# Base registers loaded later, and another order in the setup, of a graph layer on one core

## The chip, the cores and the metric

The kernel runs on one core of a Trainium2 chip. The metric is device time in microseconds (us) of one execution; before the change the median of 3 runs is 811.84 us (811.63 to 813.36).

## The reference

Nodes N = 6250, features D = 128, edges E = 206250, sorted by dst. What is computed:

```
msg = x[src] + edge_attr                      # E x D
agg = segment_sum(msg, dst, num_segments=N)   # N x D
h   = relu(agg @ W1 + b1) @ W2 + b2
h   = (h - mean(h)) * rsqrt(var(h) + eps) * ln_w + ln_b     # over the whole of h
h   = graph norm over the nodes, per feature (gn_w, gn_b, gn_ms)
out = layernorm(x + (gelu(h) + x))            # per node
```

## The kernel before, in words

**Two sums make agg.** The sum of edge_attr over dst is made by groups of 3072 edges (68 groups, each in two halves): VectorE marks which node of a window of 32 an edge goes to (`mark`, L931), TensorE multiplies marks and edges (`sum_half`, L661), ScalarE copies the sums (L529), TensorE puts them at their place among 128 columns (`turn_sums`, L675, with the table `place` that `put` makes, L943), and `add` (L955) adds them on VectorE to `agg` at a column that comes from a register. The register is loaded by `base_of(g)` (L947), a `value_load` of one word of `base_i`, on VectorE's sequencer.

The sum of x[src] is made by 25 chunks of 250 nodes. For a chunk, a matrix of counts (250 nodes by N source nodes) is built: VectorE makes five batches of marks (`mark_batch`, L1020, two tables each, three batches of buffers), TensorE counts in 25 banks of 5 products each through a ring of 4 PSUM banks (L710), ScalarE copies each bank into `counts` (L553), and when all 25 are copied TensorE multiplies 49 tiles of x, each in a high and a low part, with `counts` (L735, 98 products), and VectorE adds the result to `agg` (`add_chunk`, L1028). There is one `counts` buffer: the copies of the next chunk start after the last L735.

**Where a chunk's edges are** is looked up on the way: `stage_tile` (L880) gives a slot, GpSimd gathers `begins` from the list of edges `listed` in HBM (L449), `stage_row` (L978 to L982) gives a finer slot, GpSimd gathers `near` (L456), `make_keys` (L991 to L1005) makes keys, TensorE turns them (L690) and ScalarE copies them (L535), after which `mark_batch` may start on the chunk.

**The order** is written out by hand on every engine. The loop over pairs of chunks has on VectorE an even half and an odd half. The even half starts with `base_of` twice, then `put` twice, mark, batch 3, mark, batch 4, `add`, `make_keys`, `stage_tile`, marks, batches 0 and 1 of the next chunk, `add`, batch 2, `stage_row`, `add_chunk`. The odd half starts with `base_of` three times.

**The setup.** SyncE loads dst, then x (after src has landed), then edges. ScalarE issues the loads of the last word of each tile of 256 edges (`tile_end_i`, 805 words) and of src. VectorE and ScalarE compare the ends with the 3125 pairs of nodes (`search`, in three pieces of 4, 10 and 11 chunks, 7 comparisons each), and TensorE sums the comparisons (L633). VectorE's comparisons (piece 0) have a buffer each; ScalarE's (L508) share 3 buffers and wait for TensorE to have used them (`below_used`). VectorE packs src and dst (L893), after which ScalarE stores `listed` (L514 to L516). ScalarE splits x into its high part (L522) between pieces 1 and 2, VectorE the low part (L961).

Of the kernel before, what the change touches and what calls it, by code (L numbers as in the profile page):

```python
# [14 lines left out]
P = 128  # L15
# [54 lines left out]
EARLY = 4  # L70
BELOW = 3
# [8 lines left out]
def gnn_kernel(nc, x, src, dst, edge_attr, W1, b1, W2, b2, ln_w, ln_b, gn_w, gn_b, gn_ms, out):  # L80
# [36 lines left out]
    with ExitStack() as ctx:  # L117
# [14 lines left out]
        pair_row = nc.alloc_sbuf_tensor_at("pair_row", [P, NPAIR + 7], I16, offset=counts_at)  # L132
        x_hi = sb("x_hi", [P, NT, D], F32R)
# [11 lines left out]
        below = behind[:, 0:BELOW * SEARCH * PAIRS].rearrange("p (s v) -> p s v", s=BELOW)  # L145
# [108 lines left out]
        below_ready = sem("below_ready")  # L254
        below_used = sem("below_used")
# [228 lines left out]
        def _(act):  # L484

            act.wait_ge(rows_padded, 1)
# [6 lines left out]
            act.dma_start(src_rows[0:EVEN, :], src_full[0:EVEN, :]).then_inc(src_loaded, 16)  # L493
            act.dma_start(src_rows[EVEN:FULL, :], src_full[EVEN:FULL, :]).then_inc(src_loaded, 16)
            act.dma_start(src_rows[FULL:GROUPS, 0:REST], src_rest).then_inc(src_loaded, 16)
# [4 lines left out]
            def search(piece, sets):  # L500

                a, b = PIECES[piece]
                act.wait_ge(ends_ready, 1)
                act.wait_ge(pair_row_ready, piece + 1)
                for i in sets:
                    n = piece * SETS + i
                    act.wait_ge(below_used, max(SETS, n + 1 - BELOW))
                    nc.scalar.activation(below[:, n % BELOW, 0:(b - a) * PAIRS], pair_row[:, a * PAIRS:b * PAIRS],  # L508
                                         ACT.Sign, bias=tile_bias[:, i:i + 1]).then_inc(below_ready, 1)

            search(1, range(EARLY))
# [6 lines left out]
            search(1, range(EARLY, SETS))  # L518
# [5 lines left out]
            search(2, range(SETS))  # L524
# [99 lines left out]
        def _(pe):  # L624
            def search(piece):

                a, b = PIECES[piece]
                for i in range(SETS):
                    n = piece * SETS + i
                    pe.wait_ge(below_ready, n + 1)  # L630
                    for c in range(a, b):
                        of = first_below[:, i] if piece == 0 else below[:, n % BELOW]
# [200 lines left out]
        def _(dve):  # L833
# [23 lines left out]
            dve.wait_ge(ends_loaded, 32)  # L857
            link(dve.tensor_scalar(tile_end[:, :], tile_end_i[:, :], 1.0 / PAIR, None, ALU.mult), setup, steps)
            link(dve.tensor_scalar(tile_bias[:, :], tile_end[:, :], -1.0, -0.25, ALU.mult, ALU.add), setup, steps)
            dve.engine_nop().then_inc(ends_ready, 1)  # L860

            def search(piece):

# [465 lines left out]
```

## Time and profile before

| | |
|---|---|
| median of 3 runs | 811.84 us |
| the profiled execution's own time | 805.35 us |
| its span | 803.0 us |
| mean granted clock of TensorE | 0.963 |
| busy: TensorE, VectorE, ScalarE, GpSimd | 86%, 83%, 49%, 10% |
| VectorE's two tables of marks (L1020) | 235.8 and 184.5 us busy, 125 each |
| TensorE's products with counts (L735) | 290.6 and 287.0 us busy, 1225 each |
| ScalarE's copies of banks (L553) | 314.2 us busy, 625; idle before them 312.9 us |
| idle of VectorE before `place` (L943), ended by issue | 42.1 us |

The busy shares are means over setup (to about 62 us), 25 chunks (to about 714 us) and the two layers, norms and output behind them. The chain that ended last has TensorE with 37% of the span, VectorE 26%, issue 18% and VectorE's sequencer 7%, of which L947 alone is 4%.

### The profile page before, as it was taken

What the parts mean: (1) busy time and instruction counts of PE and PEld (TensorE: products, weight loads), DVE (VectorE), ACT (ScalarE), POOL (GpSimd) and SP (SyncE); (2) the same over time, 40 slices, a digit from 0 to 9 for tenths busy, and PEclk for the clock granted to TensorE, in tenths of its full rate; (3) what the DMA queues carried; (4) which work ended last, traced back from release to release, by engine and by line L of the source; (5) the groups of instructions that cost most, each with busy time, mean ns of one, the idle gap of its engine ahead of it and who ended that gap; (6) DMA issues with size and microseconds to landing.
All of it is one profiled execution on the core that took longest, in us unless ns stands there. A gap on an engine that the chain in (4) does not pass through costs nothing.

```text
span 803.0 us, 25641 instructions
## 1 busy us (share of the span) xinstructions
PE 688.2 (86%) x9447; PEld 620.2 (77%) x9447; DVE 667.6 (83%) x1186; ACT 396.5 (49%) x858; POOL 78.6 (10%) x68
## 2 busy tenths in 40 slices
PE   3685799998999989999899898998989989999850
PEld 3573788888888878888789887898878888788730
DVE  6765988899898988989889898898988889825585
ACT  3723365346653466434664346633565335614464
POOL 2222010101101011010101101011010110000000
PEclk9987799999999999999999999999999999999965
DMA  6858246356463563635636366363662646331005
GB/s 158 293 165 285 90 148 204 105 163 206 128 200 121 167 206 112 212 109 184 206 93 213 110 201 206 84 203 125 204 205 81 196 134 206 102 107 61 0 0 159
DMA packets 88856, 123.47 MB, mean 154 GB/s; under 512 B 8479, under 2 KB 84348, under 8 KB 88635
## 3 DMA queue, kind: packets, MB, share of 16 engines
q1 hardware_dynamic: 82220, 116.30, 45.8%
q0 software_dynamic: 5616, 5.25, 2.3%
q10 hardware_dynamic: 1000, 1.65, 0.9%
q8 instruction: 13, 0.21, 0.1%
q14 instruction: 7, 0.06, 0.0%
HBM read 119.10 MB, written 4.03 MB: 153 GB/s over the span
## 4 chain that ended last, share of the span: by engine, by line
PE 37%; DVE 26%; issue 18%; DVEq 7%; DMA 5%; ACT 5%; ACTq 1%; SPq 0%; POOLq 0%
PE bank L735 20%; DVE pool_m L1020 20%; PE bank L710 5%; PE bank L661 4%; DVEq L947 4%; PE bank L792 3%; PE bank L782 3%; ACT counts L553 2%; DVE onehot L931 2%; DMA pool_m<-in_x_dram 2%; DMA agg<-in_src_dram 1%; PE bank L633 1%; DMA begins<-listed,tile_slot 1%; DMA edges<-in_edge_attr_dram 1%; ACT x_hi L522 1%
## 5 line engine op out<-in xcount | busy, mean ns | idle before, releaser
L553 ACT CAST counts<-bank 128x490 fp32r<-128x490 f32 x625 | 314.2, 668 | 312.9 <-PE bank L710 311.4
L735 PE MATMUL bank<-counts,x_hi 128*128 128x250 f32 x1225 | 290.6, 282 | 25.5 <-ACT counts L553 25.5
L735 PE MATMUL bank<-counts,x_lo 128*128 128x250 f32 x1225 | 287.0, 279 | 0.0
L735 PEld LDWEIGHTS bank<-counts,x_hi 128*128 128x128 f32 x1225 | 231.3, 189 | 29.3 <-ACT counts L553 29.3
L1020 DVE TENSOR_TENSOR pool_m<-value_row,turned_lo 128x3328 bf16<-128x3328 bf16 x125 | 235.8, 1887 | 0.2
L735 PEld LDWEIGHTS bank<-counts,x_lo 128*128 128x128 f32 x1225 | 232.1, 190 | 0.0
L710 PE MATMUL bank<-pool_m 128*128 128x98 bf16 x3125 | 200.3, 210 | 23.1 <-DVE pool_m L1020 20.4
L710 PEld LDWEIGHTS bank<-pool_m 128*128 128x128 bf16 x3125 | 161.4, 99 | 62.1 <-ACT counts L553 43.7
L1020 DVE TENSOR_TENSOR pool_m<-value_row,turned_key 128x2548 bf16<-128x2548 bf16 x125 | 184.5, 1476 | 0.0
L661 PE MATMUL bank<-edges,onehot 128*32 128x128 f32 x3228 | 122.1, 286 | 5.2 <-DMA edges<-in_edge_attr_dram 5.2
L661 PEld LDWEIGHTS bank<-edges,onehot 128*32 128x32 f32 x3228 | 85.1, 113 | 17.9 <-DVE onehot L931 4.2
L931 DVE TENSOR_TENSOR onehot<-iota_f,dst_cols 128x384 f32<-128x384 f32 x136 | 72.7, 552 | 2.1 <-PE bank L661 1.1
L449 POOL DMA_INDIRECT begins<-listed,tile_slot x27 | 35.3, 1309 | 309.0 <-DVE tile_slot L880 287.8
L456 POOL DMA_INDIRECT begins<-listed,row_slot x27 | 32.7, 1210 | 300.1 <-DVE row_slot L982 287.9
L943 DVE TENSOR_SCALAR place<-iota_f,place_row 128x128 f32<-128x128 f32 x68 | 18.4, 295 | 42.1 <-issue 42.1
L529 ACT COPY sums<-bank 128x128 f32<-128x128 f32 x68 | 23.9, 352 | 30.4 <-PE bank L661 30.4
L633 PE MATMUL bank<-ones_b,pool_m 128*125 128x1 bf16 x175 | 20.9, 247 | 19.1 <-DVE pool_m L867 9.9
L675 PE MATMUL bank<-place,sums 128*128 128x128 f32 x136 | 31.2, 312 | 7.1 <-DVE place L943 6.4
L633 PEld LDWEIGHTS bank<-ones_b,pool_m 128*125 128x125 bf16 x175 | 19.8, 226 | 20.3 <-DVE pool_m L867 9.8
L582 ACT ACTIVATE onehot<-bank,b1c 128x250 f32<-128x250 f32 x50 | 20.7, 465 | 22.6 <-PE bank L782 22.6
L675 PEld LDWEIGHTS bank<-place,sums 128*128 128x128 f32 x136 | 21.2, 196 | 9.1 <-issue 7.5
L955 DVE TENSOR_TENSOR agg<-agg,bank 128x128 f32 x68 | 19.1, 281 | 10.2 <-PE bank L675 8.5
(151 smaller groups left out, 405.3 us busy)
## 6 DMA issues: line engine op xcount, KB each, us to landing
edges<-in_edge_attr_dram SPq DMA_DIRECT2D x134, 768.0 KB, 5.2
out_dram<-pool_m SPq DMA_DIRECT2D x6, 512.0 KB
agg<-in_dst_dram SPq DMA_DIRECT2D x1, 768.0 KB
agg<-in_src_dram ACTq DMA_DIRECT2D x1, 768.0 KB
listed<-agg ACTq DMA_DIRECT2D x1, 768.0 KB
begins<-listed,tile_slot POOLq DMA_INDIRECT x27, 7.4
begins<-listed,row_slot POOLq DMA_INDIRECT x27, 5.5
w<-in_L_gnn_W_dram SPq DMA_DIRECT2D x2, 128.0 KB, 2.8
```

What stands on the lines that cost most here:

```text
L449: pool.indirect_dma_start(begins[0:PAIRS, :], None, listed_rows, bass.IndirectOffsetOnAxis(tile_slot[0:PAIRS, 0:1], 0)).then_inc(begins_lo ...
L456: pool.indirect_dma_start(near[0:PAIRS, :], None, listed_rows, bass.IndirectOffsetOnAxis(row_slot[0:PAIRS, 0:1], 0)).then_inc(near_loaded, 16)
L553: nc.scalar.copy(counts[:, :, k * nodes:(k + 1) * nodes].rearrange("p q (i m) -> p q i m", m=PAIR), cps[k % RING][:, 0:nodes * NT].rearran ...
L633: last = nc.tensor.matmul(tile_ps[0:PAIRS, c:c + 1], of[:, (c - a) * PAIRS:(c - a + 1) * PAIRS], ones_b[:, :], start=(n == 0 and c == 0), ...
L661: last = nc.tensor.matmul(eps[s][b * WINDOW:(b + 1) * WINDOW, :], oh[:, t, :], edges[:, u, t * D:(t + 1) * D], start=(k == 0 and j == 0), ...
L675: nc.tensor.matmul(turned_sum[s], sums[:, :], place[:, s, :], start=True, stop=True).then_inc(sums_turned, 1)
L710: last = nc.tensor.matmul(cps[k % RING][:, i * KEYS:(i + 1) * KEYS], mark_lo[b % MARKED][:, n // INTER, :, n % INTER], mark_key[b % MARKED ...
L735: last = nc.tensor.matmul(sps[:, 0:CHUNK], part[:, q, :], counts[:, q, :], start=(q == 0 and part is x_hi), stop=(q == NT - 1 and part is ...
L782: last = nc.tensor.matmul(zps[u][:, k, 0:CHUNK], w1[:, k * P:(k + 1) * P], agg[:, bass.ds(c * CHUNK, CHUNK)], start=True, stop=True, skip_ ...
L931: dve.tensor_tensor(oh, window, of.to_broadcast([P, HALF, WINDOW]), ALU.is_equal).then_inc(onehot_ready, 1)
L947: return dve.value_load(base_i[0:1, bass.ds(g, 1)], min_val=0, max_val=N - 1)
L1020: last = dve.tensor_tensor(to[b % MARKED], values[:, :, 0:n, :].to_broadcast([P, BLOCKS_B, n, INTER]), of.to_broadcast([P, BLOCKS_B, n, IN ...
```

## The change

1. Loop on VectorE: `base_of` no longer stands at the head of the halves. Each load stands right in front of its `add`, the one of group first + 3 behind batch 4 of the odd half.
2. ScalarE issues the loads of src first, without a wait, and those of the tiles' ends behind them.
3. VectorE packs src and dst and releases the storing of `listed` before it touches the ends and piece 0 of the search; the storing is issued in front of ScalarE's comparisons.
4. ScalarE's 14 comparisons get a buffer each, in the room of `counts` behind `pair_row`; they no longer wait for TensorE. Both pieces stand in front of the split of x.

```diff
+        below = nc.alloc_sbuf_tensor_at("below", [P, (len(PIECES) - 1) * SETS, SEARCH * PAIRS], BF16,
+                                        offset=counts_at + (NPAIR + 7) // 16 * 32 + 32)
...
+            act.dma_start(src_rows[0:EVEN, :], src_full[0:EVEN, :]).then_inc(src_loaded, 16)
+            act.dma_start(src_rows[EVEN:FULL, :], src_full[EVEN:FULL, :]).then_inc(src_loaded, 16)
+            act.dma_start(src_rows[FULL:GROUPS, 0:REST], src_rest).then_inc(src_loaded, 16)
             act.wait_ge(rows_padded, 1)
...
-                for i in sets:
-                    n = piece * SETS + i
-                    act.wait_ge(below_used, max(SETS, n + 1 - BELOW))
-                    nc.scalar.activation(below[:, n % BELOW, 0:(b - a) * PAIRS], pair_row[:, a * PAIRS:b * PAIRS],
-                                         ACT.Sign, bias=tile_bias[:, i:i + 1]).then_inc(below_ready, 1)
-
-            search(1, range(EARLY))
+                for i in range(SETS):
+                    nc.scalar.activation(below[:, (piece - 1) * SETS + i, 0:(b - a) * PAIRS], pair_row[:, a * PAIRS:b * PAIRS],
+                                         ACT.Sign, bias=tile_bias[:, i:i + 1]).then_inc(signs_ready, 1)
+
             act.wait_ge(listed_ready, 1)
...
-            search(1, range(EARLY, SETS))
+            search(1)
+            search(2)
             act.wait_ge(x_loaded, 32)
...
-            search(2, range(SETS))
...
-                base0, base1 = base_of(first), base_of(first + 1)
                 put(first, 0, after=True)
...
-                add(first, 0, base0, c + 1)
+                add(first, 0, base_of(first), c + 1)
...
-                    add(first + 1, 1, base1, c + 1)
+                    add(first + 1, 1, base_of(first + 1), c + 1)
...
-                base2, base3, base4 = base_of(first + 2), base_of(first + 3), base_of(first + 4)
                 put(first + 3, 1)
...
-                add(first + 2, 0, base2, c + 1)
+                add(first + 2, 0, base_of(first + 2), c + 1)
                 mark_batch(c, 4)
+                base3 = base_of(first + 3)
                 put(first + 4, 0)
...
-                add(first + 4, 0, base4, c + 1)
+                add(first + 4, 0, base_of(first + 4), c + 1)
```

On VectorE the head of the even half in the loop, as instructions of the program, before (L947 is the load of a base, L943 `place`, L931 a mark, L1020 a table of a batch, L955 `add`):

```order
L1112 ISA
L947 TENSOR_LOAD base_i
L947 ISA x3
L947 TENSOR_LOAD base_i
L947 ISA x2
L942 REGISTER_ALU
L943 REGISTER_ALU
L943 TENSOR_SCALAR place<-iota_f,place_row 128x128
L943 REGISTER_ALU
L943 TENSOR_SCALAR place<-iota_f,place_row 128x128
```

and after, where lines are two or three lower, from the head to the first `add`:

```order
L941 TENSOR_SCALAR place<-iota_f,place_row 128x128
L926 ISA
L929 ISA
L929 TENSOR_TENSOR onehot<-iota_f,dst_cols 128x384
L1014 ISA
L1018 TENSOR_TENSOR pool_m<-value_row,turned_lo 128x3328
L1018 TENSOR_TENSOR pool_m<-value_row,turned_key 128x2548
L926 REGISTER_ALU
L929 ISA
L929 TENSOR_TENSOR onehot<-iota_f,dst_cols 128x384
L1014 REGISTER_ALU
L1018 TENSOR_TENSOR pool_m<-value_row,turned_lo 128x3328
L1018 TENSOR_TENSOR pool_m<-value_row,turned_key 128x2548
L945 REGISTER_ALU
L945 TENSOR_LOAD base_i
L945 ISA x2
```

The two loads stood in front of everything; the first now follows both tables of batch 4, with nothing loaded at the head.

On ScalarE the start of the program, before:

```order
L489 DMA tile_end_i<-in_dst_dram 128x6x1
L491 DMA tile_end_i<-in_dst_dram 37x1
L493 DMA agg<-in_src_dram 64x3072
L494 DMA agg<-in_src_dram 3x3072
L495 DMA agg<-in_src_dram 1x426
L497 DMA listed<-lo_i 1x118
L508 ACT_TABLE_LOAD
L508 ACTIVATE pool_m<-pair_row,tile_bias 128x1250 x4
L514 DMA listed<-agg 64x3072
L515 DMA listed<-agg 3x3072
L516 DMA listed<-agg 1x426
L508 ACTIVATE pool_m<-pair_row,tile_bias 128x1250 x3
L522 CAST x_hi<-pool_m 128x896 x7
L508 ACTIVATE pool_m<-pair_row,tile_bias 128x1375 x7
```

and after:

```order
L486 DMA agg<-in_src_dram 64x3072
L487 DMA agg<-in_src_dram 3x3072
L488 DMA agg<-in_src_dram 1x426
L492 DMA tile_end_i<-in_dst_dram 128x6x1
L494 DMA tile_end_i<-in_dst_dram 37x1
L497 DMA listed<-lo_i 1x118
L511 DMA listed<-agg 64x3072
L512 DMA listed<-agg 3x3072
L513 DMA listed<-agg 1x426
L506 ACT_TABLE_LOAD
L506 ACTIVATE below<-pair_row,tile_bias 128x1250 x7
L506 ACTIVATE below<-pair_row,tile_bias 128x1375 x7
L520 CAST x_hi<-pool_m 128x896 x7
```

The three stores of the list (`agg` holds src there) moved ahead of all comparisons, the seven comparisons of piece 2 ahead of the split of x.

## Rows read from the trace of the kernel before

**Rows 1.** Waits from 91 to 673 us: who waited for what, us in total, times, longest us.

```profile
DVE place L943 <- issue: 39.4, 23, 1.8
...
PE bank L710 <- DVE pool_m L1020: 17.5, 23, 1.2
```

**Rows 2.** Line L947, 142 to 193 us: engine, operation, ns min/median/max, starts.

```profile
L947 DVEq TENSOR_LOAD <-base_i x5: 298/301/310, 154.6 to 181.2; - x5
```

**Rows 3.** VectorE in order of time, one pair of chunks: start us, us, instruction, [idle before it].

```profile
156.74 0.29 DVE L943 TENSOR_SCALAR place<-iota_f,place_row 128x128 f32<-128x128 f32 x1 [1.80 <-issue]
...
181.99 0.48 DVE L943 TENSOR_SCALAR place<-iota_f,place_row 128x128 f32<-128x128 f32 x2 [1.60 <-issue]
...
188.33 1.48 DVE L1020 TENSOR_TENSOR pool_m<-value_row,turned_key 128x2548 bf16<-128x2548 bf16 x1
```

**Rows 4.** TensorE in the same pair of chunks, in order of time.

```profile
164.25 0.63 PE L710 MATMUL bank<-pool_m 128*128 128x98 bf16 x10 [0.38 <-DVE pool_m L1020]
...
187.92 0.86 PE L710 MATMUL bank<-pool_m 128*128 128x98 bf16 x15
...
189.93 0.64 PE L710 MATMUL bank<-pool_m 128*128 128x98 bf16 x10 [1.15 <-DVE pool_m L1020]
```

**Rows 5.** ScalarE in the even chunk of that pair, in order of time.

```profile
184.61 4.94 ACT L553 CAST counts<-bank 128x490 fp32r<-128x490 f32 x10
...
189.44 0.76 ACT L553 CAST counts<-bank 128x490 fp32r<-128x490 f32 x1
...
190.38 1.05 ACT L553 CAST counts<-bank 128x490 fp32r<-128x490 f32 x2 [0.18 <-PE bank L710]
...
191.74 1.52 ACT L553 CAST counts<-bank 128x490 fp32r<-128x490 f32 x3 [0.31 <-PE bank L710]
```

**Rows 6.** Line L947 at 50.6 to 54 us, and the table in front of that load.

```profile
L947 DVEq TENSOR_LOAD <-base_i x1: 309/309/309, 50.7 to 50.7; - x1
...
51.44 0.55 DVE L931 TENSOR_TENSOR onehot<-iota_f,dst_cols 128x384 f32<-128x384 f32 x1
```

**Rows 7.** The first 70 us, all engines, in order of time.

```profile
2.33 0.55 ACTq L493 DMA_DIRECT2D agg<-in_src_dram  x1
...
9.85 3.14 PE L633 MATMUL bank<-ones_b,pool_m 128*125 128x1 bf16 x28 [9.85 <-DVE pool_m L867]
...
13.10 1.28 ACT L508 ACT_TABLE_LOAD   x1 [13.10 <-PE bank L633]
...
14.16 3.42 DVE L893 SCALAR_TENSOR_TENSOR agg<-agg 68x426 int32<-68x426 int32 x2 [0.58 <-DMA agg<-in_src_dram]
...
17.68 0.48 ACTq L514 DMA_DIRECT2D listed<-agg  x1
...
25.60 0.67 PE L644 MATMUL bank<-ident,junk 68*128 68x68 f32 x2 [1.22 <-DVEq L909]
...
34.89 9.43 ACT L508 ACTIVATE pool_m<-pair_row,tile_bias 128x1375 bf16<-128x1375 int16 x7
...
36.38 9.32 PE L633 MATMUL bank<-ones_b,pool_m 128*125 128x1 bf16 x77 [6.34 <-ACT pool_m L508]
...
36.39 7.14 DVE L961 TENSOR_TENSOR x_lo<-pool_m,x_hi 128x896 fp32r<-128x896 f32 x7
...
45.63 4.07 PE L661 MATMUL bank<-edges,onehot 128*32 128x128 f32 x72
...
47.06 1.22 POOL L449 DMA_INDIRECT begins<-listed,tile_slot  x1 [3.02 <-DVE tile_slot L880]
...
58.05 0.47 DVE L978 TENSOR_SCALAR_CACHE_REDUCE junk<-begins,pair_w 125x256 f32<-125x256 int32 x1
```

**Rows 8.** Chain of waits in the first chunk: start us, us, what.

```profile
69.07 8.76 DMA begins<-listed,tile_slot
```

**Rows 9.** Stretches: us, then busy us (instructions) of PE, PEld, DVE, ACT, POOL; granted clock; DMA.

```profile
84.00:87.00 3.00, 2.28 (x34) 1.78 (x34) 3.00 (x4) 1.05 (x2) 0.00 (x0) 0.50 0.02 5
...
142.71:154.39 11.68, 11.68 (x102) 11.64 (x103) 11.49 (x14) 0.27 (x2) 1.28 (x1) 1.00 0.21 71
```

More of the change, by code:

```diff
@@ L69 @@
 PIECES = ((0, 4), (4, 14), (14, 25))
-EARLY = 4
-BELOW = 3
 SEARCH = 11
@@ L144, in gnn_kernel @@
         behind = pool_m[:, 2 * NT * D:MARKED * (LW + KW)]
-        below = behind[:, 0:BELOW * SEARCH * PAIRS].rearrange("p (s v) -> p s v", s=BELOW)
         first_below = behind[:, 0:SETS * PIECES[0][1] * PAIRS].rearrange("p (s v) -> p s v", s=SETS)
@@ L254, in gnn_kernel @@
         below_ready = sem("below_ready")
+        signs_ready = sem("signs_ready")
         below_used = sem("below_used")
@@ L492, in _ @@
                               dst_tiles[whole:ET, SPAN - 1:SPAN]).then_inc(ends_loaded, 16)
-            act.dma_start(src_rows[0:EVEN, :], src_full[0:EVEN, :]).then_inc(src_loaded, 16)
-            act.dma_start(src_rows[EVEN:FULL, :], src_full[EVEN:FULL, :]).then_inc(src_loaded, 16)
-            act.dma_start(src_rows[FULL:GROUPS, 0:REST], src_rest).then_inc(src_loaded, 16)
             act.wait_ge(rows_padded, 3)
@@ L498, in _, with search @@
                           ).then_inc(listed_stored, 16)
-            def search(piece, sets):
+            def search(piece):
                 a, b = PIECES[piece]
@@ L629, in search @@
                     n = piece * SETS + i
-                    pe.wait_ge(below_ready, n + 1)
+                    if piece == 0:
+                        pe.wait_ge(below_ready, i + 1)
+                    else:
+                        pe.wait_ge(signs_ready, n + 1 - SETS)
                     for c in range(a, b):
-                        of = first_below[:, i] if piece == 0 else below[:, n % BELOW]
+                        of = first_below[:, i] if piece == 0 else below[:, n - SETS]
                         last = nc.tensor.matmul(tile_ps[0:PAIRS, c:c + 1], of[:, (c - a) * PAIRS:(c - a + 1) * PAIRS],
@@ L856, in _ @@
                               ).then_inc(consts_ready, 1)
[L857 to L860, printed above, removed]
             def search(piece):
@@ L883, in _ @@
             link(dve.memset(tile_rows[:, :], 0), setup, steps)
-            search(0)
-            dve.wait_ge(below_used, SETS)
-            read_tiles(*PIECES[0])
-            dve.engine_nop().then_inc(tiles_read, 1)
-            stage_tile(0)
             dve.wait_ge(dst_loaded, 48)
@@ L897, in _ @@
             dve.engine_nop().then_inc(listed_ready, 1)
+            dve.wait_ge(ends_loaded, 32)
+            link(dve.tensor_scalar(tile_end[:, :], tile_end_i[:, :], 1.0 / PAIR, None, ALU.mult), setup, steps)
+            link(dve.tensor_scalar(tile_bias[:, :], tile_end[:, :], -1.0, -0.25, ALU.mult, ALU.add), setup, steps)
+            dve.engine_nop().then_inc(ends_ready, 1)
+            search(0)
+            dve.wait_ge(below_used, SETS)
+            read_tiles(*PIECES[0])
+            dve.engine_nop().then_inc(tiles_read, 1)
+            stage_tile(0)
             link(dve.tensor_copy(rows_f[0:GROUPS, :], rows_i[0:GROUPS, :]), setup, steps)
```

## The prediction

> **What bounds the kernel now.** I read the waits first. In the loop of chunks VectorE sits idle before `place` 23 times, 39.4 us in all, and nothing in the profile but issue ends that idle; TensorE waits for tables of marks 23 times, 17.5 us in all [rows 1]. Then the loads themselves: in one pair of chunks there are five, each 0.30 us on VectorE's sequencer [rows 2], with register operations behind each. The order in time says where they cost: VectorE idles 1.80 us at the head of the odd half and 1.60 us at the head of the even half [rows 3]. That is 3.4 us for five loads, 0.68 us each. Both idles end with `place`, so VectorE's queue was empty while the sequencer loaded.
>
> But idle time on VectorE is not time of the kernel. The next view is TensorE's order in time. It waits for marks 0.38 us in the odd half and 1.15 us in the even half, both times in front of bank 20, which needs batch 4 [rows 4]. Behind TensorE stands ScalarE, which copies the 25 banks almost without a break: ten evictions and a copy of sums take 189.44 - 184.61 = 4.83 us, so one eviction is at most 0.48 us (0.47 if I take 0.15 for the copy of sums). Around TensorE's wait this breaks: one eviction takes until 190.38 (0.94 us), the next two until 191.74 (1.36 us) [rows 5]. In between the halves TensorE's products with counts, 11.68 us, run at the full clock [rows 9], and neither ScalarE nor the next bank can start before they end. So the period of a chunk is 11.68 us of products plus ScalarE's 25 copies plus what TensorE's wait for marks puts between them. ScalarE is the floor under the count phase, VectorE the part that sticks out over it.
>
> **The loads behind tables.** Removed at the heads: 3 x 0.68 = 2.0 us (1.80 of it idle) in the odd half, 2 x 0.68 = 1.36 us in the even half. Added: the same five loads behind a batch of two tables. Is a load there free? The trace has such a place. In the setup a load starts at 50.7 us, while the table that stands in front of it in the program starts at 51.44 us [rows 6]: the sequencer ran at least one instruction ahead of the engine and loaded meanwhile. A batch is two tables, the second alone 1.48 us [rows 3], longer than 0.68 us. I take zero for the five loads; the cover is the table in front, and without it each costs 0.68 us.
>
> The Trainium skill, page "DMA: Bandwidth & Descriptors", section "Latency and other measured facts", gives a floor of about 600 ns for a `tensor_load`. The trace does not agree: 0.30 us [rows 2]. By the page's figure a load would be 0.98 us as an estimate, the first chunk below would give 2.0 us in place of 1.4, and the sum would be 0.6 us larger. The rows decide.
>
> What TensorE gains: in the even half VectorE ends batch 4 at 188.33 + 1.48 = 189.81 us [rows 3], TensorE starts on it at 189.93, 0.12 later. With 1.36 us less that is 188.57. TensorE is done with bank 19 at 187.92 + 0.86 = 188.78 [rows 4], so the wait of 1.15 us goes, with a margin of only 0.2 us. In the odd half 1.80 us come off against a wait of 0.38, so that one goes with 1.4 us to spare.
>
> What ScalarE, and so the period, gains: even half, (190.38 - 189.44 - 0.48) + (191.74 - 190.38 - 0.96) = 0.86 us, 0.89 with 0.47 [rows 5]; I take 0.87. Odd half, I take 0.35 of the 0.38 us [rows 4], since one late bank delays the copies by nearly the wait. The rest of VectorE's freed 3.2 us per pair is not lost time: it turns into a wait for the keys (`keys_ready`), which ScalarE copies at the end of its 25 banks. That is the wait that is late next.
>
> Count: the loop has 12 pairs. Even halves 1 to 11 behind the first: 11 x 0.87 = 9.6 us. Odd halves: 12 x 0.35 = 4.2 us. The last chunk has no wait of TensorE for marks, nothing. The first even half is different: nothing is running ahead there, VectorE has just waited for a gather (8.76 us to landing, [rows 8]), then come the two loads, then batch 3, for which TensorE waits. There all 2 x 0.68 = 1.4 us come off. Sum of the loads: 15.2 us. Bounds: no more than all of TensorE's waits, 17.5 us [rows 1], plus 1.4; no less than half of the two main terms, 7, plus 1.4, if VectorE regains only part of its idle.
>
> **The setup.** src: issued at 2.33 us before [rows 7], now ScalarE's first work, some 1.6 us earlier, where the ends were. Its landing ends at 14.16, when packing starts [rows 7]. It shares the DMA engines with dst, whose last rows are issued as before, so I take 0.9 us of the 1.6: packing starts at 13.3 (12.6 to 14.1). The ends land behind src now, which is no cost as long as they land by 16.7.
>
> From there: packing 3.42 us to 16.7, against 17.6. ScalarE then issues three stores (1.3 us, in steps like the 0.48 of the first), loads its table (1.28 us), and makes the comparisons without a break: 7 of 1250 columns at about 1.25 us, scaled from the 9.43 us of the 7 of 1375 [rows 7], to 28.1 us, then 9.43 us to 37.5. VectorE makes piece 0 meanwhile; TensorE's 28 products for it are 3.14 us [rows 7]. Its next work, from packing's end to the transposes, took 25.60 - 17.6 = 8.0 us, and starts now 4.6 us later than packing's end, so TensorE can transpose at 29.3, not 25.60, about when piece 1 is done (28.1 + 1.3). The transposes take 4.4 us, to 33.9. Piece 2 then needs no ScalarE: TensorE's own pace is 3.14/28 = 0.112 us, 77 x 0.112 = 8.6 us, to 42.5; at the pace seen, 9.32 us [rows 7], to 43.2. The sums of the first groups start there, not at 45.63: 3.1 us (2.4) earlier, and the loads of the next edges with them, since they wait for these sums.
>
> Against that: the split of x now comes last on ScalarE, 37.5 us, so VectorE's low parts run 38.4 + 7.14 = 45.5 us, not to 43.5, and `make_keys` follows them [rows 7]. The first slot of chunk 1 is staged 2.1 us later, at 48.1, its gather leaves at 49.2 instead of 47.06 [rows 7]. A gather of this kind landed in 8.76 us [rows 8], and this one by 58.05 at the latest, where no wait stands in front of L978, so in 6 to 8.8 us; VectorE wants it at about 55.2 (58.05 [rows 7] less 2.9), and it lands between 55.2 and 58.0. So the path through gathers is late by 0 to 2.8 us and the gain of 2.9 shrinks. I take 2.2 us for the setup, bounds 0 and 4 (if src lands all of 1.6 us earlier).
>
> The waits removed by own buffers save nothing by themselves: TensorE kept pace with ScalarE in piece 2 (9.32 beside 9.43 us, [rows 7]). The move of pieces ahead of the split is what counts.
>
> **Sum.** 9.6 + 4.2 + 1.4 + 2.2 = 17.4 us. The profiled execution's own time 805.35 becomes 787.9; the median of the runs shown, 6.5 us above it, becomes 811.84 - 17.4 = 794.4 us.
>
> **Rivals.**
> - *The loads are exposed where they now stand* (the sequencer cannot run past a table). Then each costs 0.68 us behind its table. In the odd half batch 4 comes 1.80 - 0.68 earlier, still enough for 0.38. In the even half the loads stand behind batch 4, but the one behind batch 1 of the next chunk delays `add_chunk` by 0.68, so batch 4 is 0.5 us late and the gain per even half about 0.4. That makes 11 x 0.4 + 4.2 + 1.4 + 2.2 = 12.2 us, 799.6 us. The load that ran ahead speaks against it [rows 6].
> - *The freed time does not reach ScalarE*: another wait (keys, a gather, the slot of the ring) takes the place of TensorE's. Gain by the setup, the first chunk and a third of the loop, 2.2 + 1.4 + 4.6 = 8.2 us: 803.6 us. For it: the margin in the even half is 0.2 us. Against it: the long waits of the loop name no gather and no DMA, only issue and marks [rows 1].
> - *The setup costs what it gains*, through the late gather: 796.6 us. For it: the landing may take the whole 8.8 us.
> - *Slower, by the clock.* TensorE's granted clock is 0.50 at 84 to 87 us, that is 1.2 GHz, and 1.00, 2.4 GHz, in the products with counts [rows 9]. In the first chunk TensorE sits with gaps. If the new order of gaps left it at the lower level through two whole chunks, each set of products would take 11.68 us more and the count phase some 7 more: 2 x 18.7 - 17.4 = 20 us slower, 831.8 us. It decides from one chunk on (18.7 against 17.4). Against it: the gaps of the first chunk keep their order and get shorter. The Trainium skill's page "TensorE: Matmul & The Clock Gate", section "HAM oscillation — how this bites in real kernels", says that waits between bursts of products can bring the clock down again; by it the time would be the same 831.8 us; the trace agrees in that the level is low at 84 to 87 us.
>
> **How the numbers follow.** Forecast 0.70, exposed loads 0.08, time not reaching ScalarE 0.09, setup giving nothing 0.09, the clock 0.02, other 0.02. The forecast's own range, with the bounds of loads and setup, is 790 to 798; reaching to the first and third rival gives 789 to 801. About 0.2% (1.6 us) is what a measurement of this kernel can tell from no change. Faster by more than that: 0.95; the same: 0.02; slower: 0.03.
>
> **What would show it.** Right: VectorE's idle before `place` falls from 39.4 to under 8 us; TensorE's wait for marks from 17.5 to under 3; a pair of chunks takes about 1.2 us less; the loads lie beside running tables; VectorE shows a new wait in front of batch 0, for ScalarE. In the setup the sums of edges start at 42 to 43.5 us, and the split ends after 43. Wrong: idle of 0.7 us behind each batch (first rival), ScalarE's copies with gaps as before (second), a stall at L978 in the setup larger than 2 us (third), L735 at half clock (fourth).

## The result, and the profile after

The change takes **807.7 us** (median of 7 runs, 805.54 to 809.16), the kernel before beside it 811.87 us (811.63 to 813.36): ratio 0.994, 95% interval 0.9931 to 0.995. That is 4.2 us faster where 17.4 were forecast, and outside the range.

The profile after says at first that everything forecast has happened. Waits from 91 to 673 us (who waited for what, us in total, times, longest us), beside [rows 1]:

```profile
DVE pool_m L1018 <- PE bank L710: 22.1, 23, 1.2
PE bank L710 <- ACT counts L550: 15.3, 21, 0.9
DVE pool_m L1018 <- ACT turned_key L532: 14.7, 22, 0.8
...
DVE place L941 <- issue: 2.2, 11, 0.3
```

VectorE's idle before `place` is 2.2 us instead of 39.4; TensorE no longer waits for tables of marks (17.5 before); VectorE waits for the keys ScalarE copies (L532), as forecast. But there are two new waits: VectorE for TensorE, and TensorE for ScalarE to free a bank. And the pair of chunks, whose halves are told apart by ScalarE's long wait, takes 200.67 to 226.26 to 251.91, 51.24 us, where in the profile of before it took 50.6. By these two profiles the loop is slower than the one it replaces.

Where it goes is seen at the head of the count phase. The profile after, all engines, in order of time:

```profile
200.67 1.05 ACT L550 CAST counts<-bank 128x490 fp32r<-128x490 f32 x2 [11.68 <-PE bank L710]
...
201.24 1.45 POOL L456 DMA_INDIRECT begins<-listed,row_slot  x1 [11.81 <-DVE row_slot L980]
...
201.59 1.12 PE L710 MATMUL bank<-pool_m 128*128 128x98 bf16 x20
202.66 1.05 ACT L550 CAST counts<-bank 128x490 fp32r<-128x490 f32 x2 [0.94 <-PE bank L710]
202.73 0.37 SPq L362 DMA_DIRECT2D edges<-in_edge_attr_dram  x1
202.80 1.89 DVE L1018 TENSOR_TENSOR pool_m<-value_row,turned_lo 128x3328 bf16<-128x3328 bf16 x1 [1.18 <-PE bank L710]
```

TensorE's products for bank 2 start at 201.59, 0.92 us into the phase, as they did before. But ScalarE may copy bank 2 only at 202.66, SyncE may load edges only at 202.73, VectorE may write its table only at 202.80. Three engines that wait for TensorE get its releases at the same moment, and that is when GpSimd's issue of the gather of `near` ends (201.24 + 1.45 = 202.69). I call it a **hold**: releases of TensorE that arrive when GpSimd has issued its gather. "Bank 2 at" is in what follows the time from ScalarE's first copy of a phase to its copy of bank 2: 1.99 us here; it was 1.36 in every phase but the last (1.31) of the profile of before.

### The profile page after: what moved, and what is told of

Same layout as the page of the kernel before. It is cut to its first block, busy times and chain, and to the rows that moved or that the text cites. A ratio compares the mean times of both kernels' runs of the same rounds, so it can differ in the third digit from the quotient of the medians.

```text
span 804.2 us, 25636 instructions
## 1 busy us (share of the span) xinstructions
PE 690.7 (86%) x9447; PEld 620.9 (77%) x9447; DVE 669.9 (83%) x1186; ACT 393.5 (49%) x858; POOL 82.0 (10%) x68
## 4 chain that ended last, share of the span: by engine, by line
PE 70%; ACT 14%; issue 7%; DVE 3%; DMA 3%; ACTq 1%; DVEq 1%; SPq 0%; POOLq 0%
PE bank L735 36%; PE bank L710 14%; ACT counts L550 12%; PE bank L661 9%; PE bank L792 3%; PE bank L782 3%; PE bank L633 2%; PE bank L675 2%; DMA edges<-in_edge_attr_dram 1%; DMA agg<-in_dst_dram 1%; DMA begins<-listed,tile_slot 1%; ACT sums L526 1%; DVE pool_m L1018 1%; PE bank L819 1%; ACT pool_m L617 1%
## 5 line engine op out<-in xcount | busy, mean ns | idle before, releaser
L710 PE MATMUL bank<-pool_m 128*128 128x98 bf16 x3125 | 203.6, 211 | 22.9 <-ACT counts L550 15.7
L456 POOL DMA_INDIRECT begins<-listed,row_slot x27 | 36.1, 1337 | 316.4 <-DVE row_slot L980 303.6
L526 ACT COPY sums<-bank 128x128 f32<-128x128 f32 x68 | 25.9, 381 | 28.5 <-PE bank L661 28.5
L1195 DVE TENSOR_SCALAR agg<-bank,par 128x250 f32 (+1 forms) x25 | 11.9, 478 | 18.3 <-PE bank L792 18.2
L782 PE MATMUL bank<-agg,w 128*128 (+1 forms) x100 | 25.1, 375 | 0.8 <-DVEq L1188 0.8
L792 PE MATMUL bank<-onehot,w 128*128 128x250 f32 x100 | 25.4, 376 | 0.1
```

The costliest lines, as they stand in the source:

```text
L456: pool.indirect_dma_start(near[0:PAIRS, :], None, listed_rows, bass.IndirectOffsetOnAxis(row_slot[0:PAIRS, 0:1], 0)).then_inc(near_loaded, 16)
L526: nc.scalar.copy(sums[:, :], eps[s]).then_inc(sums_copied, 1)
L710: last = nc.tensor.matmul(cps[k % RING][:, i * KEYS:(i + 1) * KEYS], mark_lo[b % MARKED][:, n // INTER, :, n % INTER], mark_key[b % MARKED ...
L782: last = nc.tensor.matmul(zps[u][:, k, 0:CHUNK], w1[:, k * P:(k + 1) * P], agg[:, bass.ds(c * CHUNK, CHUNK)], start=True, stop=True, skip_ ...
L792: last = nc.tensor.matmul(hps[u][:, 0:CHUNK], w2[:, k, :], hidden[:, u, k, :], start=(k == 0), stop=(k == HC - 1))
```

## The experiments

Five jobs were run, each on a chip of its own, called A to E; each has its own runs of the kernel before, and within a job they agree. For the runs and the profiles shown before the experiments the chip isn't known. Two numbers tell a profile's loop: bank 2 at (odd, even half), and the time from the first to the last of the 24 count phases behind the first chunk. They come from ScalarE's copies in order of time.

| kernel | chip | bank 2 at | first to last phase | median us | before there |
|---|---|---|---|---|---|
| before, as shown above | | 1.36, 1.36 | 582.2 | 805.35 (its own) | |
| the change, as shown | | 1.99, 2.27 | 588.5 | 807.7 | 811.9 |
| e1_loop | A | 1.36, 1.36 | 571.8 | 794.0 | 805.6 |
| e2_setup | A | 1.36, 1.36 | 583.5 | 803.8 | 805.6 |
| e3_ownsem | A | 1.36, 1.36 | 572.2 | 790.8 | 805.6 |
| e4_pool | A | 1.36, 1.36 | 572.3 | 790.4 | 805.6 |
| r_after | B | 1.98, 2.27 | 588.8 | 808.8 | 812.9 |
| e6_nop | B | 1.99, 2.26 | 588.7 | 808.75 | 812.9 |
| e7_sem | B | 1.96, 2.26 | 589.0 | 808.2 | 812.9 |
| e0_before | B | 2.00, 2.17 | 588.7 | 815.5 (one run) | 812.9 |
| r2_after | C | 1.98, 2.25 | 588.7 | 809.0 | 812.1 |
| r2_loop | C | 1.99, 2.19 | 588.0 | 810.1 | 812.1 |
| r2_ownsem | C | 1.99, 2.27 | 588.5 | 807.0 | 812.1 |
| r2_pool | C | 1.36, 1.36 | 571.9 | 790.8 | 812.1 |
| r3_after | D | 1.98, 2.27 | 588.5 | 808.2 | 811.4 |
| g1_before_pool | D | 1.36, 1.36 | 582.3 | 805.2 | 811.4 |
| g2_iota | D | 1.36, 1.36 | 572.7 | 791.8 | 811.4 |
| g3_twice | D | 2.11, 2.27 | 595.4 | 816.05 | 811.4 |
| r4_after | E | 1.36, 1.36 | 571.9 | 791.05 | 805.2 |
| r4_pool | E | 1.36, 1.36 | 572.1 | 789.2 | 805.2 |

**Loop or setup (e1_loop, e2_setup).** e1 is the kernel before with the loads moved and nothing else, e2 the change with the loads back at the heads:

```diff
-                base0, base1 = base_of(first), base_of(first + 1)
...
-                add(first, 0, base0, c + 1)
+                add(first, 0, base_of(first), c + 1)
...
```

Expected of e1:

> The kernel before with part 1 alone (the loads of bases in front of their adds). In the changed kernel ScalarE's copy of bank 2 starts 2.0 to 2.3 us after its copy of bank 0 in 22 of 24 count phases, 1.36 us in the kernel before, and a pair of chunks takes 51.24 us, not 50.62. Theory A (the loads' new place alone does this, since VectorE now arrives early and waits for banks_done): here too, a pair of chunks at 51.2 us, so the loop is 12 x 0.6 = 7 us longer, less 1.4 us in the first chunk: the profiled execution's own time near 811. Rival B (the setup's new order leaves the loop in another rhythm): a pair at 49.5 us as forecast, some 12 to 15 us faster than before in the profile.

Expected of e2:

> The changed kernel with the loads of bases back at the heads of the halves. Theory A: bank 2 at 1.36 us, a pair of chunks at 50.6 us, and the products with counts of the first chunk start about 4.2 us earlier than 92.03 (at 87.8): own time of the profiled execution near 801, the fastest so far. Rival B: the loop stays at 51.2 us per pair, near 808.

Measured on chip A: e1 0.9845 (0.9818 to 0.9872) of before, 11.6 us faster; e2 0.998 (0.9966 to 0.9993), 1.8 us faster (its even halves take 25.53 us, 0.1 more than before). The parts alone give 13.4 us, on a chip where no release is late. So neither part brings the hold by itself, and I still took it for something that only the whole has.

**An own semaphore, a later gather (e3_ownsem, e4_pool).** In e3 VectorE waits on a semaphore of its own, `batches_used`, that TensorE's products raise; in e4 VectorE waits as in the change, and GpSimd issues the gather of `near` only when the first batch of the phase is used:

```diff
...
-dve.wait_ge(banks_done, c * BANKS + ((b - MARKED + 1) * BPB + CREDIT))
+dve.wait_ge(batches_used, c * BATCHES + (b - MARKED + 1 + BATCHES))
```

```diff
 def gather_near(c, after=None):
     pool.wait_ge(row_staged, c + 1)
+    if after is not None:
+        pool.wait_ge(batches_used, after)
...
```

> The changed kernel, with VectorE's waits for free mark buffers moved to a semaphore of their own (raised by the first product behind a batch), so that ScalarE alone waits for banks_done. Theory A1 (two engines that wait for one semaphore hold each other up): ScalarE starts bank 2 at 1.36 us, the wait in front of batch 4 is gone, a pair of chunks near 49.5 us, own time near 786 to 790. Rival A2 (it is the time at which VectorE and GpSimd work beside TensorE, not the semaphore): bank 2 stays at 2.0 to 2.3 us, a pair at 51.2 us, own time near 806.

> The changed kernel, where GpSimd issues the gather of near only when the first batch of the count phase is used (its own semaphore), some 2.3 us after ScalarE's first copy instead of 0.6 to 0.9; VectorE still waits on banks_done. In the changed kernel the late starts of ScalarE, SyncE and VectorE end at about the time when GpSimd's issue ends (2.03 us in the odd half), and the two phases with normal starts are those in which GpSimd issued late (1.17 and 1.58 us). Theory A2 (GpSimd's issue of the gather delays what TensorE's release wakes): bank 2 at 1.36 us, a pair of chunks 49.5 to 50.2 us. Rival A1 (the shared semaphore): bank 2 stays at 2.0 to 2.3 us, a pair at 51.2 us.

Measured on chip A: e3 0.9806 (0.9787 to 0.9826), e4 0.9809 (0.9792 to 0.9827), 15 us faster than before, both with bank 2 at 1.36. Two different edits with the same effect are suspicious: either both cure, or there was nothing to cure on this chip. The unaltered change didn't run beside them, so this experiment can't say.

**Is it the program at all (r_after, e6_nop, e7_sem, e0_before).** The whole change again, beside it the change with one more `sem_inc` on TensorE ahead of its loop (e6), the change with `signs_ready` declared last, so that all semaphores behind it keep their numbers of before (e7), and the kernel before with a profile:

```diff
 pe.wait_ge(x_split, NT // PIECE)
+pe.sem_inc(spare, 1)
 with pe.Fori(0, PAIRED) as p:
```

```diff
-signs_ready = sem("signs_ready")
...
 out_stored = sem("out_stored")
+signs_ready = sem("signs_ready")
```

> The changed kernel once more, unaltered, beside the others. In its first profile ScalarE's bank 2 came 2.0 to 2.3 us after bank 0 in 22 of 24 count phases, where the loop alone, the own semaphore and the late gather all show 1.36 us. Theory C (the late releases belong to this one program: its setup, its semaphores and its moments together): again 2.0 to 2.3 us, a pair of chunks at 51.2 us, no more than 1% faster than before. Rival D (it came from the load or chip of that job, where the kernel before took 811.9 us and not 805.6): bank 2 at 1.36 us, a pair at 49.7 us, own time near 790, some 15 us faster than before.

> The changed kernel with one more instruction on TensorE's sequencer in front of the loop (a release of a semaphore that nobody waits for), so that all that follows lies one instruction further. Theory E (the place of the instructions decides the late releases): bank 2 at 1.36 us and a pair of chunks at 49.7 us, if the unaltered one stays at 51.2. Theory C or rival D: as the unaltered one.

> The changed kernel with the new semaphore signs_ready declared last, so that banks_done, halves_free and all others have the numbers that they have in the kernel before. If the semaphores' numbers decide the late releases: bank 2 at 1.36 us, a pair of chunks at 49.7 us, if the unaltered one stays at 51.2. Otherwise as the unaltered one.

> The kernel before, once more with a profile. Its profile of the first job has an own time of 805.35 us beside a median of 811.87 without one. If late releases come and go by the load of a program, this look may show some of its 24 count phases with bank 2 at 2 us or later and a longer pair of chunks than 50.62 us; if not, bank 2 at 1.36 us throughout and an own time near 805.

Measured on chip B: 0.9939 (0.9915 to 0.9962), 0.9943 (0.9925 to 0.996), 0.9949 (0.9931 to 0.9967); all three held, neither the place of the code nor the number of a semaphore matters. The profile of the unaltered kernel before settled more than the three. In order of time, beside [rows 3] for its even half:

```profile
182.26 1.05 ACT L553 CAST counts<-bank 128x490 fp32r<-128x490 f32 x2 [11.74 <-PE bank L710]
183.09 1.21 POOL L456 DMA_INDIRECT begins<-listed,row_slot  x1 [11.64 <-DVE row_slot L982]
183.18 1.12 PE L710 MATMUL bank<-pool_m 128*128 128x98 bf16 x20
...
184.44 2.00 ACT L553 CAST counts<-bank 128x490 fp32r<-128x490 f32 x4 [1.13 <-PE bank L710]
```

and its waits from 91 to 673 us:

```profile
DVE place L943 <- issue: 39.4, 23, 1.8
...
PE bank L710 <- DVE pool_m L1020: 2.1, 11, 0.4
```

The kernel before is held too on this chip, bank 2 at 2.18. It still has the loads' 39.4 us of idle on VectorE, but TensorE's wait for marks is 2.1 us instead of 17.5: **the hold has already taken the wait that the change removes.** So the hold doesn't come with the change. It comes with the job and its chip, which these runs don't tell apart, and it was missing in the one profile of before that the prediction read. Below, "a chip that holds" means the chip of such a job.

**The same kernels on a holding chip (r2_after, r2_pool, r2_ownsem, r2_loop).**

> The whole change, unaltered, a second time. Theory chip (late releases at the head of a count phase come with the chip of the job, whatever the kernel): if the kernel before stands at 805 to 807 us here, this stands at 789 to 793 us, ScalarE's copy of bank 2 follows bank 0 by 1.36 us and a pair of chunks takes 49.7 us; if before stands at 811 to 814 us, this stands at 806 to 810 us, bank 2 at 1.98 and 2.27 us, the pair at 51.2 us. Theory program (the change itself brings the late releases): 807 to 809 us and bank 2 at 1.98 and 2.27 us on either kind of chip.

> The change, with GpSimd's gather of near issued only when the first batch is used (2.7 us into the phase), a second time. Theory gather (on a chip with late releases they last until GpSimd has issued its gather; no gather there, no late release): 789 to 793 us on either kind of chip, bank 2 at 1.36 us. Theory chip alone (the releases are late there whatever GpSimd does): about 807 us where before stands at 812.

> The change, with VectorE waiting on a semaphore of its own instead of the banks' count, a second time. Theory gather: as the unaltered change of this job (808 us where before stands at 812, 790 where before stands at 806). Theory shared semaphore (the third waiter on one semaphore makes its updates late): 789 to 793 us in either case.

> The kernel before with the loads of the bases alone moved behind tables, a second time. Theory chip: 793 to 795 us where before stands at 806, and 811 to 814 us (no gain at all, pair of chunks 51.2 us) where before stands at 812. Theory program: 794 us in either case.

Measured on chip C: 0.9955 (0.994 to 0.997), **0.9725 (0.9693 to 0.9757)**, 0.9941 (0.9924 to 0.9959), 0.9972 (0.9957 to 0.9986). The own semaphore cures nothing; the later gather cures all of it, and as TensorE raises that semaphore in both versions, raising it isn't the cure. The loads alone, worth 11.6 us on chip A, are worth 2.0 us here; expected was nothing. The cured phase, r2_pool:

```profile
201.06 1.06 ACT L555 CAST counts<-bank 128x490 fp32r<-128x490 f32 x2 [11.68 <-PE bank L715]
...
202.42 1.05 ACT L555 CAST counts<-bank 128x490 fp32r<-128x490 f32 x2 [0.30 <-PE bank L715]
202.88 1.89 DVE L1027 TENSOR_TENSOR pool_m<-value_row,turned_lo 128x3328 bf16<-128x3328 bf16 x1 [0.87 <-PE bank L715]
...
203.50 3.94 ACT L555 CAST counts<-bank 128x490 fp32r<-128x490 f32 x8
203.80 2.06 POOL L459 DMA_INDIRECT begins<-listed,row_slot  x1 [13.64 <-PE bank L715]
...
204.19 0.64 PE L715 MATMUL bank<-pool_m 128*128 128x98 bf16 x10
```

The gather leaves 2.2 us later into the phase and its issue now takes 2.06 us, beside VectorE's tables, and none of that costs anything: 571.9 us from the first to the last phase, as on chip A. ScalarE even copies eight banks without a gap across the issue, among them banks whose products TensorE starts only at 204.19. Whether an issue that lies under a running table holds nothing, or its hold falls between two releases, the rows don't tell.

**What in the gather holds, and does before pay too (g1_before_pool, g2_iota, g3_twice, r3_after).** g1 is the edit of e4 on the kernel before. g2 has the later gather and in its old place an operation that moves nothing by DMA; g3 issues the gather twice, at the old place:

```diff
+pool.iota(spare[:, :], [[1, P], [0, INTER]], base=0, channel_multiplier=0,
+          allow_small_or_imprecise_dtypes=True).then_inc(spare_done, 1)
 pool.wait_ge(batches_used, after)
```

```diff
                                         ).then_inc(near_loaded, 16)
+    pool.indirect_dma_start(near2[0:PAIRS, :], None, listed_rows,
+                            bass.IndirectOffsetOnAxis(row_slot[0:PAIRS, 0:1], 0)
+                            ).then_inc(near2_loaded, 16)
```

> The kernel before, with GpSimd's gather of near issued only once TensorE has used the first batch. Theory gather (TensorE's releases are held while GpSimd issues the gather, and before has this too): where the unaltered kernel before stands at 812 us, this stands at 804 to 807 us, ScalarE's copy of bank 2 at 1.36 us, the pair of chunks at 50.6 us instead of 51.2; where before stands at 806, this is the same within 2 us. Theory change (only the changed kernel suffers from the gather): 811 to 813 us where before stands at 812.

> The change with the gather issued after the first batch, and in the gather's old place an operation of GpSimd that moves nothing by DMA (an iota of 256 columns, 1.5 us in the setup's trace). Theory issue (what holds the releases is the issue of the indirect transfer): as without the iota, 789 to 793 us, bank 2 at 1.36 us. Theory engine (any work of GpSimd there holds them): 805 us or more, bank 2 at 2.0 us and later.

> The change with the gather of near issued twice in a row, the second into a tile of its own that nobody reads. Theory issue, where before stands at 812 us: the releases are held until the second issue ends, bank 2 at 3.2 us or later, a pair of chunks 1.5 to 2.5 us longer than the change's 51.2, in all 825 to 840 us; where before stands at 806: 790 to 796 us. Theory data (the transfer's traffic, not its issue, holds them): some 0.2 us more in each phase, 808 to 814 us.

> The whole change, unaltered, beside these. Where before stands at 812 us: 807 to 809 us, bank 2 at 1.98 and 2.27 us. Where before stands at 806 us: 789 to 793 us, bank 2 at 1.36 us, the pair of chunks at 49.7 us.

Measured on chip D: g1 0.9921 (0.9905 to 0.9938), so before pays 6.2 us for the hold at the head of its phases; g2 0.9749 (0.9731 to 0.9767); g3 1.0054 (1.0038 to 1.0071); r3 0.9955 (0.9938 to 0.9971). In g1 the later issue still holds, and it costs nothing:

```profile
206.83 1.56 ACT L558 CAST counts<-bank 128x490 fp32r<-128x490 f32 x3
207.13 1.22 POOL L459 DMA_INDIRECT begins<-listed,row_slot  x1 [13.30 <-PE bank L715]
207.19 1.88 DVE L1029 TENSOR_TENSOR pool_m<-value_row,turned_lo 128x3328 bf16<-128x3328 bf16 x1
...
208.57 3.43 ACT L558 CAST counts<-bank 128x490 fp32r<-128x490 f32 x7 [0.17 <-PE bank L715]
```

Bank 7 is copied at 208.57, 1.44 us behind the issue's start and 4.19 us into the phase; in the profile of before it is copied at 3.83. The loop stays as long as there (582.3 us from first to last phase against 582.2): TensorE's waits for marks fall from 17.5 to 8.1 us, and waits of 9.0 us for ScalarE stand in their place. So moving the gather takes the hold away from where it costs; that it takes the hold itself away is not shown.

In g2 the iota lies where bank 2 is released, and bank 2 comes at 1.36:

```profile
199.98 1.05 ACT L563 CAST counts<-bank 128x490 fp32r<-128x490 f32 x2 [11.71 <-PE bank L723]
...
201.06 1.51 POOL L462 IOTA spare<- 128x256 bf16 x1 [10.49 <-DVE row_slot L997]
...
201.34 1.05 ACT L563 CAST counts<-bank 128x490 fp32r<-128x490 f32 x2 [0.32 <-PE bank L723]
...
201.85 1.88 DVE L1035 TENSOR_TENSOR pool_m<-value_row,turned_lo 128x3328 bf16<-128x3328 bf16 x1
```

In this phase the iota starts only 0.28 us ahead of bank 2, but VectorE's table, 0.79 us behind that start, is on time too, and in the other phases the iota starts 0.9 to 1.4 us ahead of bank 2, which stays at 1.36. So it isn't any work of GpSimd. In g3 a second hold follows the first in the even halves:

```profile
229.92 1.06 ACT L555 CAST counts<-bank 128x490 fp32r<-128x490 f32 x2 [11.75 <-PE bank L715]
...
230.83 1.21 POOL L458 DMA_INDIRECT begins<-listed,row_slot  x1 [12.38 <-DVE row_slot L985]
...
232.18 0.58 ACT L555 CAST counts<-bank 128x490 fp32r<-128x490 f32 x1 [1.20 <-PE bank L715]
232.34 1.21 POOL L461 DMA_INDIRECT near<-listed,row_slot  x1 [0.30 <-issue]
...
233.69 1.89 DVE L1023 TENSOR_TENSOR pool_m<-value_row,turned_lo 128x3328 bf16<-128x3328 bf16 x1 [2.13 <-PE bank L715]
```

Bank 2 is released between the two issues, VectorE's table only behind the second. I had expected one long hold and 825 to 840 us; it is two, and what slips through between them makes it 816.05, 7.9 us above the change. Most even halves take 26.20 us instead of 25.65. In the odd halves the second issue starts under a running table, takes 2.9 us and delays nothing that can be seen; their 0.13 us more come from the first issue, which starts at 0.71 us instead of 0.57. At the head of a phase each issue holds for itself.

**The unaltered change on a chip that doesn't hold (r4_after, r4_pool).**

> The whole change, unaltered, once more. Where before stands at 812 us: 807 to 809 us, bank 2 at 1.98 and 2.27 us. Where before stands at 806 us (a chip that doesn't hold the releases): 789 to 793 us, bank 2 at 1.36 us, the pair of chunks at 49.7 us.

> The change with the gather of near issued after the first batch, on another chip: 789 to 793 us on either kind of chip.

Chip E doesn't hold. The change takes 791.05 us (790.42 to 792.04), 0.982 (0.9802 to 0.9839) of before, **14.1 us faster**; the version with the later gather 789.2 us, 0.9804 (0.9784 to 0.9825). r4_after, the same head of a phase as in the first fence of order:

```profile
199.60 1.06 ACT L550 CAST counts<-bank 128x490 fp32r<-128x490 f32 x2 [11.68 <-PE bank L710]
...
200.18 1.46 POOL L456 DMA_INDIRECT begins<-listed,row_slot  x1 [11.49 <-DVE row_slot L980]
...
200.96 1.05 ACT L550 CAST counts<-bank 128x490 fp32r<-128x490 f32 x2 [0.30 <-PE bank L710]
201.43 1.89 DVE L1018 TENSOR_TENSOR pool_m<-value_row,turned_lo 128x3328 bf16<-128x3328 bf16 x1 [0.88 <-PE bank L710]
```

Same kernel, same gather at the same place with the same 1.46 us of issue, and no hold. The version with the later gather takes the same on both kinds of chip: 790.4, 790.8 and 789.2 us on A, C and E, where before takes 805.6, 812.1 and 805.2. Against the change it gains 18.1 us on C; on E its loop is no faster (572.1 against 571.9 us), and the medians lie 1.9 us apart with runs that overlap.

## Why the prediction was wrong, and where it was right

**The step that failed** is the last line of the sum: "the median of the runs shown, 6.5 us above it, becomes 811.84 - 17.4". I took the 6.5 us between the profile's own time and the median as an offset that any kernel carries. It is the hold: 588.7 us from first to last phase on chip B against 582.2 in the profile shown, 6.5 us. The profiled execution and the median belonged to different regimes of the loop, and a gain read in one was taken off the other. Beside it two terms of the sum were mis-sized: without hold the change gives 14.1 us, not 17.4.

**Why the hold takes the whole gain of the loop.** A half takes ScalarE's chain, 24.98 us odd and 24.74 even when nothing stands in its way (r4_after). The hold sits at the head of that chain, so it adds in full: 24.98 + (1.99 - 1.36) = 25.61 and 24.74 + (2.28 - 1.36) = 25.66; measured in the profile after are 25.59 and 25.65. In the kernel before, the loads make VectorE late for batch 4, and the hold makes ScalarE and TensorE late by more: 24.98 + (1.97 - 1.36) = 25.59, 24.74 + (2.18 - 1.36) = 25.56, measured 25.59 and 25.55 in the halves of e0_before from 156.67 us on. Two delays in parallel, of which the longer counts. On a holding chip both kernels stand on the same floor, and what is left is the setup.

| term | forecast | without hold (E) | with hold |
|---|---|---|---|
| even halves, each | 0.87 | 25.43 - 24.74 = 0.69 | 0 |
| odd halves, each | 0.35 | 25.20 - 24.98 = 0.22 | 0 |
| loop, first to last phase | 13.8 | 582.2 - 571.9 = 10.3 | 588.7 - 588.5 = 0.2 |
| first even half and setup | 3.6 | 92.03 - 88.21 = 3.8 | |
| whole | 17.4 | 14.1 | 3.1 to 4.2 |

Point by point:

- *Loads behind tables are free*: right. VectorE's idle before `place` went from 39.4 to 2.2 us, on either kind of chip. The load itself stays at 0.30 us, with its register operations behind it.
- *ScalarE is the floor*: right, and it was the key to the hold too. *TensorE's waits go, margin 0.2 us in the even half*: right, on chip E none is left among the long waits.
- *0.87 per even half* was mis-sized. I took from ScalarE's gaps 0.48 us per copy, start to start. But the products wait for the end of the last copy, and six copies in a row need 3.13 us to it, not 2.88. Before, from 189.44 to 193.26, the end of the last copy, it took 3.82 [rows 5]; 3.82 - 3.13 = 0.69. r4_after:

```profile
184.46 3.13 ACT L550 CAST counts<-bank 128x490 fp32r<-128x490 f32 x6
187.24 0.52 ACT L532 CAST turned_lo<-bank 128x125 bf16<-128x125 f32 x1
```

- *0.35 per odd half* was mis-sized likewise: the 11 last copies went from 5.71 to 5.52 us. TensorE's wait of 0.38 us had met a ScalarE that still had a bank to copy.
- *Setup*: its steps nearly right, its sum too low rather than too high. In r4_after packing starts at 13.95 (13.3 forecast), the sums of edges at 42.70 (42.5 to 43.2), the low parts end at 39.02 + 7.10 = 46.1 (45.5), the gather of chunk 1 leaves at 49.65 (49.2) and lands in 7.36 (6 to 8.8), its slot is staged at 57.04 (55.2 to 58.0):

```profile
13.95 3.42 DVE L882 SCALAR_TENSOR_TENSOR agg<-agg 68x426 int32<-68x426 int32 x2 [7.45 <-DMA agg<-in_dst_dram]
...
42.70 3.43 PE L661 MATMUL bank<-edges,onehot 128*32 128x128 f32 x72
...
49.65 1.22 POOL L449 DMA_INDIRECT begins<-listed,tile_slot  x1 [3.02 <-DVE tile_slot L875]
...
57.04 0.48 DVE L976 TENSOR_SCALAR_CACHE_REDUCE junk<-begins,pair_w 125x256 f32<-125x256 int32 x1 [0.87 <-DMA begins<-listed,tile_slot]
```

  Not foreseen: packing waits for dst now, not for src ([rows 7] name src), so the rest of src's 1.6 us can't be had.
- *The first even half, 1.4 us by the two loads*: right. From the landing of the gather to VectorE's first table behind it, e2, with the loads at the heads, takes 3.48 us and e1, with the loads moved, 1.98:

```profile
73.09 0.48 DVE L976 TENSOR_SCALAR_CACHE_REDUCE junk<-begins,pair_w 125x256 f32<-125x256 int32 x1 [3.73 <-DMA begins<-listed,tile_slot]
...
76.55 1.88 DVE L1018 TENSOR_TENSOR pool_m<-value_row,turned_lo 128x3328 bf16<-128x3328 bf16 x1
```

```profile
79.88 0.48 DVE L978 TENSOR_SCALAR_CACHE_REDUCE junk<-begins,pair_w 125x256 f32<-125x256 int32 x1 [3.65 <-DMA begins<-listed,tile_slot]
...
81.83 1.89 DVE L1020 TENSOR_TENSOR pool_m<-value_row,turned_lo 128x3328 bf16<-128x3328 bf16 x1
```

  All four profiles with the loads at the heads have 3.48 to 3.58 us there, fifteen of the sixteen others 1.98 (g2, with its iota, 3.21). From the landing to the products with counts it is 14.20 to 14.37 us against 12.50 to 13.48 (g2 13.92). The setup's gain is the earlier landing itself: 78.6 us on average in the five profiles with the old setup, 74.7 in the fifteen with the new one, 3.9 us where 2.2 were forecast; e2 gains less in all (1.8) since its loop is 1.3 us longer. The landings of the new setup spread from 72.5 to 78.4 us, and the first phase behind them starts from 96.98 to 102.88, so one pair of profiles tells the setup's gain to some us only. Where that spread comes from stays open.
- *Rivals*: the one that "the freed time does not reach ScalarE" came true on the holding chips, three of five and that of the result, at 0.09 and 803.6 us. It left a third of the loop's gain; there was almost none (0.2 of 13.8 us). Its mechanism was another: none of keys, gather landing or ring slot, but the release of bank 2. The clock stayed at 0.96 on average and the loads weren't exposed.
- *What would show it* asked for "ScalarE's copies with gaps as before"; it is a gap at another place, at the head of the phase.
- *The range*: 790 to 798 us is narrower than the bounds it cites. Loads of 8.4 to 18.9 us and a setup of 0 to 4 give 788.9 to 803.4 us. The 807.7 lie outside that too.

**What stays open.** Why some jobs hold and some don't: each ran once, on one chip, so the chip and whatever else differs between jobs weren't told apart. Which of the two regimes a profile belongs to is known only for its own execution. And what exactly is held. TensorE's records show the products start on time (0.92 us in both), but their ends are modelled, so the records can't say whether TensorE's writes or only its signals are late. That ScalarE, SyncE and VectorE get them within 0.14 us of each other in the odd half speaks for one cause behind TensorE; in the even half, though, SyncE loads edges at 1.63 us, late by 0.4 but 0.65 ahead of ScalarE's bank 2, so not all releases wait for one moment.

## What to carry to other kernels

A gain is to be taken off the execution it was read in. Where the profiled execution and the median of the runs differ by more than the runs among themselves (6.5 us here, the three runs 1.7), the profile shows another regime than the one that is timed: find the difference first. Before a wait is removed, ask whether another delay runs beside it; after its removal the longer of the rest counts. And it pays to try another place for an indirect transfer issued by GpSimd than the moment at which the engine that sets the pace hangs on a fresh release of TensorE: here 2.2 us later cost nothing and gave 18.1 us on a chip that holds (808.95 to 790.82), 6.2 in the kernel before.

## What the runs showed of the hardware

- On chips B, C and D releases by TensorE came 0.6 to 0.9 us late at the head of a phase beside GpSimd's issue of an indirect transfer. Where the issue starts 0.57 us into the phase, bank 2 is at 1.98; from 0.92, at 2.27; from 1.17, bank 2 is on time and VectorE's release comes at 2.55 to 2.59 instead of about 1.82; from 1.58, nothing is late. So the hold begins 0.24 to 0.44 us behind the issue's start (1.58 lets a release at 1.82 through, 0.92 holds one due at 1.36) and ends some 1.31 to 1.46 behind it. The last phase is an exception: issue at 0.85, bank 2 at 1.48. On A and E the same issue held nothing, and on C and D none is seen where the issue starts under a running table (r2_pool, g2_iota).
- The issue of one gather takes 1.21 us. One that starts while VectorE makes marks ends 1.08 to 1.10 us behind that instruction's end: 1.46 us in r4_after (issue from 200.18, a mark until 200.55), 2.06 in r2_pool (issue from 203.80, a table until 204.77). A table that starts behind the issue doesn't lengthen it: 1.22 us in g1, with the table 0.06 us later. The Trainium skill, page "DMA: Bandwidth & Descriptors", section "SWDGE vs HWDGE vs iDMA", says that GpSimd writes descriptors into SBUF, and that VectorE locks it out of there while it runs in a mode that uses two ports. The trace agrees in that the issue waits for VectorE; in which mode the marks run, no row shows.
- It goes the other way too: beside g2's iota, VectorE's `place` took 1.47 us, where it takes 0.28 alone (200.87 us in the profile after):

```profile
201.06 1.51 POOL L462 IOTA spare<- 128x256 bf16 x1 [10.49 <-DVE row_slot L997]
...
201.19 1.47 DVE L958 TENSOR_SCALAR place<-iota_f,place_row 128x128 f32<-128x128 f32 x1
```

  This cost nothing there (24.8 and 25.0 us per half), since VectorE has time to spare in the changed kernel.
